# Two changes to a Perceiver block: how decay weights and value heads are made in the cross attention, and how many buffers the experts' split weights have

## The reference

```python
# L0 cross attention: 32 heads of 8, the context has 2048 rows per batch
q = x @ Wq.T;  k_raw = context @ Wk.T;  v_raw = context @ Wv.T
kv = concat([k_raw, v_raw], -1).reshape(b, m, 32, 8, 2);  k, v = kv[..., 0], kv[..., 1]
out = softmax(rmsnorm(q) @ rmsnorm(k).T * 8 ** -0.5) @ v

# L1 summary of the same context: a decaying sum over its rows
K = sigmoid(decay);  x = kv @ W_in.T + b_in
s_t = K * s_(t-1) + x_t;   summary = mean over t of (s_t @ W_out.T + b_out)

# L1 experts: 16 experts (width 176, top 4), and a shared one of width 704
combine = top-4 of softmax(x @ gate_w.T), normalised
shared = (silu(g) * u) @ shared_down.T * sigmoid(x @ shared_gate_vec.T)
for each expert: acc += (silu(x @ Wg.T) * (x @ Wu.T)) @ w_d.T * combine[:, e]
```

## Time and profile before

| | |
|---|---|
| median of 3 timed runs | 408.24 us (407.4 to 408.91) |
| profiled execution, its own time | 406.9 us |
| its span | 405.3 us |
| PE busy | 374.2 us, 92% |
| DVE busy | 329.2 us, 81% |
| ACT busy | 267.6 us, 66% |
| POOL busy | 221.5 us, 55% |
| PE's clock | 9 (90% or more of full speed) in all 40 slices |

### The profile page before, as it was taken

One profiled execution on the slowest core, in us unless ns is written; L12 is line 12 of the kernel. 1 busy time (PEld: TensorE's weight loads), 2 busy tenths in 40 slices (PEclk: granted clock), 3 DMA queues, 4 the chain that ended last, 5 costly groups with the idle time before them and its releaser, 6 DMA issues.

```text
span 405.3 us, 14183 instructions
## 1 busy us (share of the span) xinstructions
PE 374.2 (92%) x5863; PEld 288.4 (71%) x5863; DVE 329.2 (81%) x736; ACT 267.6 (66%) x554; POOL 221.5 (55%) x286
## 2 busy tenths in 40 slices
PE   7889989999999999889999999989889987799996
PEld 4456656666666767679989897778778864567775
DVE  7788989997799998768999996787997677866663
ACT  3588888897988898975545533822999246345532
POOL 2566577766566666016544430630399746999500
PEclk9999999999999999999999999999999999999999
DMA  5647641652311100570000017120000391000000
GB/s 165 234 136 247 225 140 44 185 158 69 113 40 38 35 25 4 158 287 2 2 0 2 1 46 313 32 112 1 2 2 2 123 392 62 2 1 2 2 0 27
DMA packets 10832, 34.77 MB, mean 86 GB/s; under 512 B 2193, under 2 KB 7313, under 8 KB 8977
## 3 DMA queue, kind: packets, MB, share of 16 engines
q1 hardware_dynamic: 10624, 33.86, 24.3%
q10 hardware_dynamic: 144, 0.00, 0.0%
HBM read 33.60 MB, written 0.26 MB: 84 GB/s over the span
## 4 chain that ended last, share of the span: by engine, by line
PE 51%; DVE 23%; POOL 10%; issue 9%; ACT 4%; DMA 1%; SPq 0%; DVEq 0%; POOLq 0%; ACTq 0%
PE ps L1897 9%; PE ps L1264 6%; PE ps L1855 5%; PE ps L1246 5%; PE ps L1884 3%; PE ps L1867 3%; PE ps L975 3%; PE ps L957 3%; PE ps L473 2%; PE ps L916 2%; POOL sb_w_ri L1696 2%; PE ps L923 2%; ACT sb_arena L1805 2%; DVE sb_big L654 2%; PE ps L534 1%
## 5 line engine op out<-in xcount | busy, mean ns | idle before, releaser
L1805 ACT ACTIVATE sb_arena<-ps 128x1024 f32<-128x1024 f32 x128 | 123.7, 1019 | 12.1 <-PE ps L1884 11.7
L1897 PE MATMUL ps<-sb_arena 128*25 128x128 f32 (+1 forms) x2048 | 68.7, 274 | 0.3 <-ACT sb_arena L1805 0.3
L1897 PEld LDWEIGHTS ps<-sb_arena 128*25 128x25 f32 (+1 forms) x2048 | 50.3, 97 | 7.5 <-ACT sb_arena L1805 1.0
L1855 PE MATMUL ps<-sb_w_ri 128*32 128x512 f16 x768 | 47.3, 379 | 3.0 <-DVE sb_arena L1602 1.8
L563 POOL TENSOR_TENSOR sb_halves<-sb_big,sb_halves 128x256 fp32r<-128x256 f32 x28 | 21.6, 792 | 43.7 <-ACT sb_halves L547 43.7
L1687 POOL TENSOR_TENSOR sb_big<-sb_arena 128x256 f32<-128x256 f32 x30 | 18.7, 623 | 45.3 <-DVE sb_arena L1563 45.3
L1855 PEld LDWEIGHTS ps<-sb_w_ri 128*32 128x32 f16 x768 | 21.5, 97 | 17.3 <-POOL sb_w_ri L1696 3.8
L1175 POOL TENSOR_TENSOR sb_mid<-sb_mid 128x512 f32<-128x512 f32 x16 | 21.9, 1376 | 20.3 <-DVE sb_mid L1075 20.2
L1338 ACT ACTIVATE sb_arena<-ps 128x176 f32<-128x176 f32 x40 | 12.5, 318 | 29.7 <-PE ps L1264 29.7
L1264 PE MATMUL ps<-sb_theta 128*128 128x352 f16 x168 | 26.9, 312 | 3.3 <-DVE sb_theta L1424 2.3
L1443 DVE SCALAR_TENSOR_TENSOR sb_arena<-ps,sb_w_q,sb_arena 128x176 f32<-128x176 f32 x40 | 15.4, 395 | 17.7 <-ACT sb_arena L1338 17.5
(11 more groups left out here) (269 smaller groups left out, 929.6 us busy)
## 6 DMA issues: line engine op xcount, KB each, us to landing
sb_arena<-in_ctx SPq DMA_DIRECT2D x32, 128.0 KB, 2.6
sb_mid<-in_w_down SPq DMA_DIRECT2D x1, 3584.0 KB, 11.4
sb_big<-in_w_gu SPq DMA_DIRECT2D x1, 3520.0 KB, 11.1
sb_mid<-in_w_ffn SPq DMA_DIRECT2D x3, 768.0 KB, 5.2
sb_big<-in_w_gu SPq DMA_DIRECT2D x1, 2112.0 KB, 7.8
sb_big<-in_w_q SPq DMA_DIRECT2D x2, 1024.0 KB, 5.9
sb_big<-in_w_k SPq DMA_DIRECT2D x2, 1024.0 KB, 6.8
sb_big<-in_w_v SPq DMA_DIRECT2D x2, 1024.0 KB, 5.6
```

Source lines behind the costliest of these rows:

```text
L1805: nc.scalar.activation(probs[:, n % P_SLOTS].rearrange("p a g n -> p a (g n)"), ps[:, bank:bank + 2], ACT.Exp, scale=XD ** -0.5).then_inc( ...
L1855: i = T.matmul(ps[r:r + 32, 7], ctx_half[:, t % 2, c, kt, r:r + 32], wkv_half[:, d, kt], start=(n + kt == 0), stop=(n == 2 and kt == KT - ...
L1897: i = T.matmul(ps[32 * gg:32 * gg + m, 6, j * P:(j + 1) * P], v_sb[:, t % V_SLOTS, 4 * gg + j, head], probs[:, n % P_SLOTS, a, gg], start= ...
```

## The change

Decay weights: at the start one scan makes the powers K^1 to K^128 in `powers` (start value 1, addend 0), another makes block 0 as before. Every later block is one `scalar_tensor_tensor`: powers times the last weight of the block before, plus block 0. Of the sums only three are left (powers, block 0, and the last weights of blocks 0 to 14); the second attention step puts them together with two small instructions. SP waits for three sums and not for sixteen.

Values: `take_v` is one copy of 256 elements with an output pattern of two runs of heads, where it was two copies of 128.

Experts: four slots for split weights, the fourth in a free part of `w_q4`, and FIRST = 4: POOL scales and subtracts for one more unit, DVE makes 16 low halves and not 17, each one unit earlier; ACT makes the fourth high half after the layer norm's root. In PE's order `turn(n)` is followed by `down(n - 2)`, so that `down(11)`, `down(12)` and `down(13)` follow the last turn.

```diff
+GEO_SUMS = 3
+        powers = x_pairs[:, 2560:2560 + P]
@@ sync
-            sp.wait_ge(sem("geo_summed"), MB)
+            sp.wait_ge(sem("geo_summed"), GEO_SUMS)
@@
         gu_half = [a.rearrange("p (c k n) -> p c k n", c=2, k=KT) for a in (
-            pairs[:, 1024:2432], pairs[:, 2432:3840], w_q4[:].rearrange("p k n -> p (k n)")[:, 512:1216].bitcast(F16))]
-        FIRST = 3
+            pairs[:, 1024:2432], pairs[:, 2432:3840], w_q4[:].rearrange("p k n -> p (k n)")[:, 512:1216].bitcast(F16),
+            w_q4[:].rearrange("p k n -> p (k n)")[:, 1216:1920].bitcast(F16))]
+        FIRST = SLOTS = 4
@@ vector_attention
-                    dve.wait_ge(sem("geo_summed"), MB)
-                    V.tensor_reduce(gsum[:], gsums[:], AX_X, ALU.add).then_inc(sem("u_ready"), 1)
+                    dve.wait_ge(sem("geo_summed"), GEO_SUMS)
+                    step(dve, V.tensor_scalar(gsums[:, 3:4], gsums[:, 1:2], float(MB), None, ALU.mult))
+                    V.scalar_tensor_tensor(gsum[:], gsums[:, 0:1], gsums[:, 2:3], gsums[:, 3:4], ALU.mult, ALU.add
+                                           ).then_inc(sem("u_ready"), 1)
@@ tensor_experts
-                        if turned >= 2:
+                        if turned >= 3:
                             down(summed)
                             summed += 1
@@ unit_high (and gu_half[u % SLOTS] everywhere)
-            if u >= 3:
-                act.wait_ge(sem("gu_projected"), B * (u - 2))
+            if u >= SLOTS:
+                act.wait_ge(sem("gu_projected"), B * (u - SLOTS + 1))
@@ scalar_experts
-            for u in range(FIRST):
+            for u in range(FIRST - 1):
                 unit_high(act, u)
             ln_rstd(act, LN_OF["moe"])
+            unit_high(act, FIRST - 1)
@@ decay_weights(t)
-                first = geo[:, t * P - 1:t * P] if t else 0.0
-                V.tensor_tensor_scan(geo[:, t * P:(t + 1) * P], dec[:, 2:3].to_broadcast([P, P]),
-                                     ones[:, 0:1].to_broadcast([P, P]), first, ALU.mult, ALU.add
-                                     ).then_inc(sem("geo_ready"), 1)
+                if t == 0:
+                    step(dve, V.tensor_tensor_scan(powers, dec[:, 2:3].to_broadcast([P, P]),
+                                                   xnT[:, 0, 0, 0:1].to_broadcast([P, P]), 1.0, ALU.mult, ALU.add))
+                    i = V.tensor_tensor_scan(geo[:, 0:P], dec[:, 2:3].to_broadcast([P, P]),
+                                             ones[:, 0:1].to_broadcast([P, P]), 0.0, ALU.mult, ALU.add)
+                else:
+                    i = V.scalar_tensor_tensor(geo[:, t * P:(t + 1) * P], powers, geo[:, t * P - 1:t * P], geo[:, 0:P],
+                                               ALU.mult, ALU.add)
+                i.then_inc(sem("geo_ready"), 1)
@@ sum_weights(n)
-                V.tensor_reduce(gsums[:, n:n + 1], geo[:, n * P:(n + 1) * P], AX_X, ALU.add).then_inc(sem("geo_summed"), 1)
+                of = (powers, geo[:, 0:P], geo[:, 0:(MB - 1) * P].rearrange("p (t n) -> p t n", n=P)[:, :, P - 1])[n]
+                V.tensor_reduce(gsums[:, n:n + 1], of, AX_X, ALU.add).then_inc(sem("geo_summed"), 1)
@@ take_v(t)
-                for r in range(2):
-                    i = V.tensor_copy(v_sb[:, t % V_SLOTS, :, 25 * r:25 * r + 8],
-                                      ps[:, 7, 256 + 128 * r:384 + 128 * r].rearrange("p (h d) -> p h d", d=XD))
-                i.then_inc(sem("kv_taken"), 1)
+                a = v_sb[:, t % V_SLOTS]
+                both = bass.AP(tensor=a.tensor, offset=a.offset, ap=[a.ap[0], [25, 2], [VP, 16], [1, XD]])
+                V.tensor_copy(both, ps[:, 7, 256:512].rearrange("p (r h d) -> p r h d", r=2, d=XD)
+                              ).then_inc(sem("kv_taken"), 1)
@@ vector loop over tiles
-                    else:
+                    elif t + 2 < MB + GEO_SUMS:
                         sum_weights(t + 2 - MB)
```

More of the change, by code:

```diff
@@ L1263, in tensor_experts @@
                     for kt in range(KT):
-                        i = T.matmul(ps[:, 2 + k % 4, 0:2 * EI], xe_half[:, c, kt, b * P:b * P + P], gu_half[u % 3][:, d, kt],
+                        i = T.matmul(ps[:, 2 + k % 4, 0:2 * EI], xe_half[:, c, kt, b * P:b * P + P], gu_half[u % SLOTS][:, d, kt],
                                      start=(n + kt == 0), stop=(n == 2 and kt == KT - 1))
@@ L1295, in unit_high @@
                 act.wait_ge(sem("late_gu_loaded"), 16)
-            nc.scalar.activation(gu_half[u % 3][:, 0], unit_weights(u), ACT.Copy, scale=1.0 if u < FIRST else W_SCALE
+            nc.scalar.activation(gu_half[u % SLOTS][:, 0], unit_weights(u), ACT.Copy, scale=1.0 if u < FIRST else W_SCALE
                                  ).then_inc(sem("gu_high"), 1)
@@ L1309, in pool_experts @@
                 pool.wait_ge(sem("gu_high"), u + 1)
-                G.tensor_tensor(gu_half[u % 3][:, 1], unit_weights(u), gu_half[u % 3][:, 0], ALU.subtract
+                G.tensor_tensor(gu_half[u % SLOTS][:, 1], unit_weights(u), gu_half[u % SLOTS][:, 0], ALU.subtract
                                 ).then_inc(sem("first_low"), 1)
@@ L1423, in unit_low @@
                 dve.wait_ge(sem("gu_high"), u + 1)
-                V.scalar_tensor_tensor(gu_half[u % 3][:, 1], unit_weights(u), W_SCALE, gu_half[u % 3][:, 0], ALU.mult,
+                V.scalar_tensor_tensor(gu_half[u % SLOTS][:, 1], unit_weights(u), W_SCALE, gu_half[u % SLOTS][:, 0], ALU.mult,
                                        ALU.subtract).then_inc(sem("gu_low"), 1)
```

## The result

The changed kernel takes 403.21 us (median of 4 runs, 402.34 to 404.09) against 407.82 (4 runs of the kernel before on the same chip): ratio 0.9888, 95% interval 0.9864 to 0.9911. Timed a second time, on another chip, it took 404.29 against 408.22: 0.9909 (0.9881 to 0.9937). By the two ratios the change is worth -3.7 and -4.6 us (their intervals reach from -2.6 to -5.5); forecast were -4.5 and 403.7. The profiled execution (404.09, span 402.5) is the slowest of its four, so the two profiles stand only 2.8 us of span apart.

What follows compares the result with a forecast made beforehand. PE, busy 92% of the span, was taken as the bound, so only its waits could give time back. Start +0.45, weights -1.37, values -0.1 and experts -3.5 sum to -4.5: 408.24 to 403.7 us, range 401.6 to 406.2.

Steps and rivals of the forecast that it cites:

- The start: Start of the cross attention: a third weights instruction makes the query sums late, +0.45 us (ends +0.2 and +0.9).
- The weights in the tiles: Cross attention tiles: 0.13 us saved in eight tiles, 0.11 in three, sum -1.37 us (ends 0 and -1.8).
- L1694 goes back to 0.40. So 0.13 per tile: Cross attention, first batch: POOL's context split L1694 shortens from 0.53 to 0.40 us, so 0.13 per tile.
- key copies 4.62 apart in tiles 5, 6, 9 to 14: Sign in the cross attention's first batch: period between key copies falls from 4.75 to 4.62 us in these tiles.
- The values: Cross attention tiles: one copy instead of a pair, worth 0.06 us where PE leads (tiles 7 and 15), -0.1 us.
- The fourth slot: Experts: PE finishes steps 10 and 11 before the first down projection, -1.83 us.
- The projections one pair later: Experts: a 0.34 us wait goes at six places, -2.04 us; 0.4 us allowed back for late H.
- No gain in the loop: Cross attention rival: the new form holds the port as long as the scan; 405.1 us, chance 0.18.
- DVE as the experts' pace: Experts rival: H late behind a stretched low half, six small waits move to the steps; 405.4 us, chance 0.10.
- The fourth, better: Rival: all 14 tiles gain (-1.8), start costs only 0.2, no step waits for H; 402.6 us, chance 0.07.
- The order at the port: Cross attention rival: DVE's L1583 reaches the port before POOL's L1707; 412.1 us if in all 25 tiles, chance 0.05.

Runs made afterwards that it cites:

- e2: Kernel before with the decay weights by powers and the values in one instruction, experts untouched: 407.31 us, ratio 0.9988.
- e10: Kernel before with the decay weights by powers alone, values still a pair of copies, experts as before: 407.20 us, ratio 0.9990.
- e11: Changed kernel with the queries' sums first and ten more filling matmuls on PE around the first key transposes: 402.45 us, ratio 0.9873.
- e12: e11 with POOL's product with the weights waiting for DVE's key scaling in tiles 9 to 12 alone: 402.02 us, ratio 0.9859.
- e6: Changed kernel without the decay weights of tiles 2 to 15, those of tiles 0 and 1 used in turn: 402.10 us, ratio 0.9858.
- e5: Kernel before with one edit, the values of a tile copied by one instruction: 407.15 us, ratio 0.9980.
- e4: Kernel before with the fourth slot and fourth first unit alone, down projections as before: 407.41 us, ratio 1.0002.
- e1: Kernel before with the expert edits alone (four slots, four first units, products one pair later): 403.33 us, ratio 0.9892.
- e9: Changed kernel with POOL's product with the weights waiting for DVE's key scaling from tile 2 on: 403.99 us, ratio 0.9909.
- e7: Changed kernel with the queries' sums ahead of the first two tiles' weights, their scaling ahead of the second's: 403.73 us, ratio 0.9887.

## Why the prediction was right, and where it was not

The total was right, and partly by luck, since two errors cancel: the cross attention was to bring -1.0 and brought -0.5 by its time and 0 to -0.4 by the traces (from the start of the weights' split to key copy 31 it is 152.13 us before, 151.93 in e2, 151.76 in e10, 152.17 and 151.84 after); the experts were to bring -3.5 and brought -4.0 by trace, -4.4 by time.

*The start (+0.45).* The mechanism held: the third instruction met POOL's subtract and lasted 0.59, between the bounds of 0.28 and 0.66. Counted from the start of the weights' split, the key copy of tile 2 is 13.23 and 13.05 us away in the changed kernel, 13.09 in e2, and 12.67 before: +0.4 to +0.6. In e10, where POOL's instructions stand otherwise to DVE's, it is 12.79. Putting the sums first removes all of it in e11 (12.61), but only part in e12 (12.91), which starts with the same code.

*The weights in the tiles (-1.37).* This term was mis-sized. The claim "L1694 goes back to 0.40. So 0.13 per tile" failed: it went to 0.46, and the tile gave 0.07. The 0.14 for the rest of the new instruction behind the port was right, and the prediction even placed its end behind the start of the cast; it took that remaining overlap for none. What it added up was the gain of having no such instruction at all, which e6 measures: 4.62. The 4.75 was also taken for more tiles than have it: before, the periods of tiles 9, 10 and 11 are 4.83, 5.10 and 5.10, since POOL packs queries there, so "key copies 4.62 apart in tiles 5, 6, 9 to 14" could not have come about. They gained the same 0.06 to 0.07 nevertheless, and so did tile 7, which was to gain nothing; tiles 8 and 15 gained nothing, as forecast. The three intervals from key copy 2 to 5, which the forecast gave 0.11 each, gave 0.08, 0.06 and -0.14: in the third PE's key projection starts 1.52 ahead of the key copy that it releases (33.62 and 35.14), as before (32.90 and 34.42), and DVE stands idle for it for 0.08, so that one waits for PE. Sum -0.5 to -0.7. The Trainium skill's rule in "SBUF — State Buffer", section "Who interferes with whom", against which the prediction weighed this part, is borne out as far as contention goes: the new instruction lasts 0.34 at 50.19 in the changed kernel's first profile, where POOL is idle, and 0.59 beside POOL's square. What the prediction drew from it, that the period would stay at 4.75, did not come.

*The values (-0.1).* Nothing in the tiles, swallowed at the port (e5).

*The fourth slot (-1.83).* The right amount of time went, in half by the wrong edit. The prediction said under the slot that "What changes is that PE has finished steps 10 and 11 by 348.95"; that is the lag's doing, and e4, with the slot alone, still waits 2.08 there. That the two waits for low weights are no gain by themselves was right: in e4 they became waits for H. With the lag PE does two steps of 0.895 and one turn of 0.44 ahead of the first projection which it did behind it before:

```profile
350.31 1.95 PE L1264 MATMUL ps<-sb_w_q,sb_theta 128*128 128x352 f16 x12
352.10 0.60 PE L1233 MATMUL ps<-sb_id,sb_arena 128*128 128x128 f32 x4
```

With these added for the kernel before, the way from the first H to the first projection is 11.59 + 1.79 + 0.44 = 13.82 before, 12.83 with the lag, 11.92 with both: -1.9, of which 1.0 is the lag's and 0.9 the slot's.

*The projections one pair later (-2.04, and 0.4 allowed for late H).* From the first projection to the end, with the same steps and turn taken off: 53.13 - 1.79 - 0.44 = 50.90 before, 48.83 with both edits: -2.07, nearly the -2.04 forecast. All six small waits went (8.87 for 9.21), no step waits for H after the first projection in the changed kernel, and the 0.4 allowed for it was not used. That allowance is the term that was mis-sized: with it at nothing the experts' forecast would have been -3.9, and -4.0 was measured.

*The rivals.* No gain in the loop: half true, 0.07 of the 0.13. DVE as the experts' pace: excluded by e1 and by the changed kernel, where no step waits for H after the first projection. The fourth, better, had the experts right (-3.9) and the tiles wrong (-1.8). The order at the port stayed as it was in the changed kernel, though closer (77.32 ahead of 77.37, 0.05 and not 0.11). When forced by a wait in e9 it cost nothing in sum, and not 7 us in the tiles: the rival's price took no account of POOL's idle 1.35 us before each square, of which 0.56 was left in e9.

## What to carry to other kernels

When an instruction overlaps another at a port, its worth is not its length but how far it pushes the end of what closes the loop; a kernel with the instruction left out gives the ceiling at once. Before a saving is booked to a buffer, look which edit changes the order in front of the wait: here one comparison (`turned >= 3`) carried three quarters of the experts' gain by trace (3.1 of 4.0 us; 2.6 of 4.4 by time), and the fourth buffer was worth 0.9 us on top and nothing alone. When work moves across a landmark, count all of it: two steps and a turn here. A single profile can carry 1.6 us of clock at its start; compare landmarks from one fixed instruction to another.

## What was not expected of the hardware

The granted clock fell to 0.50 (1.2 GHz, the lower of the two levels) for some 3 us in the profiles of e5 and e7 (from 18.4 and 18.6) and e1 (from 19.8), and stayed at 1.00 (2.4 GHz) in the others with the same work. PE had been busy 1.62, 1.76 and 2.18 of the 3 us from 15 to 18 in e5, e7 and e1, but only 1.48 in the kernel before, whose clock stayed up: the rows at hand don't tell why it falls in one execution and not in the next. In e5 and e7 it fell at the end of PE's idle stretch of 1.13 us in front of the first scores, in e1 0.8 us after it; the kernel before and the changed kernel have the same stretch without a fall. The third key projection (24 matmuls) took 2.75 us in e5 and e7 and 2.39 in e1, against 1.48. In the first profile of the changed kernel the clock fell within 334 to 335, and PE had been busy 0.67 and 0.98 of the two us ahead; the second profile has 1.00 from 333 to 339. And an instruction in front of a contended one, the values copy here, can be shortened with no effect at all: the next one waits longer at the port (0.72 for 0.66).
